# A post-norm transformer layer on eight cores: activation loads issued by ScalarE instead of GpSimd, and a scalar chain written as one row

## The reference

```python
# x: (8, 2048, 1024) f32, one sequence per core
# 1. causal attention with a low-rank K and V, then residual and layernorm
q = (x @ wq)                      # 8 heads of 128
k_lat = x @ wk_down; v_lat = x @ wv_down     # 2 KV heads, latent width 32
k = k_lat @ wk_up; v = v_lat @ wv_up
y = softmax(causal(q k^T / sqrt(128))) v     # 4 query heads share a KV head
x = layernorm(x + y @ wo)
# 2. six nodes, each with three edges and full attention of 8 heads
nodes = {-1: x}
for c in range(6):
    q = ew[c,0] * (nodes[in_q] @ We[eq] + be[eq])
    k = ew[c,1] * (nodes[in_k] @ We[ek] + be[ek])
    v = ew[c,2] * (nodes[in_v] @ We[ev] + be[ev])
    o = softmax((q Wq)(k Wk)^T / sqrt(128)) (v Wv) @ Wo
    nodes[c] = act_w[c] * o + q
# 3.
x = layernorm(x + layernorm(nodes[5]) * g + b)
```

## Time and profile before

| | |
|---|---|
| two runs | 7837.41 and 7932.83 us, median 7885.12 us |
| profiled execution | 7838.38 us, slowest core's span 7837.3 us |
| the eight cores' spans | 7800.0 to 7837.3 us |
| busy in the span: TensorE | 5592.8 us (71%) |
| ScalarE, VectorE | 2477.1 us (32%), 1753.2 us (22%) |
| mean granted TensorE clock | 0.852 of 2.4 GHz |
| DMA: issued by GpSimd (q0), by SyncE (q1) | 224.67 MB, 42.76 MB |

### The profile page before, as it was taken

One profiled execution on the slowest core, in us unless ns is written; L12 is line 12 of the kernel. 1 busy time (PEld: TensorE's weight loads), 2 busy tenths in 40 slices (PEclk: granted clock), 3 DMA queues, 4 the chain that ended last, 5 costly groups with the idle time before them and its releaser, 6 DMA issues.

```text
span 7837.3 us, 67298 instructions; the slowest of 8 cores (7800.0 to 7837.3 us)
## 1 busy us (share of the span) xinstructions
PE 5592.8 (71%) x21825; PEld 2141.0 (27%) x22250; DVE 1753.2 (22%) x2522; ACT 2477.1 (32%) x2138; POOL 127.8 (2%) x161
## 2 busy tenths in 40 slices
PE   6455668677886777867778967779777779656654
PEld 3111123222332223322223422224222234212211
DVE  2432222111112112131112131111311112332233
ACT  1123402454123452115440134431144511224322
POOL 0000000000000000000000000000000000000000
PEclk9577878899997998979898979989889989778777
DMA  3000031000330002310003300113200023000000
GB/s 81 11 27 27 17 91 33 17 11 11 70 65 6 19 15 49 97 27 11 11 11 81 76 16 11 22 38 76 54 17 11 11 59 94 10 17 11 27 27 22
DMA packets 112503, 271.76 MB, mean 35 GB/s; under 512 B 5216, under 2 KB 30112, under 8 KB 112182
## 3 DMA queue, kind: packets, MB, share of 16 engines
q0 software_dynamic: 98768, 224.67, 12.9%
q1 hardware_dynamic: 13414, 42.76, 1.6%
HBM read 286.55 MB, written 67.11 MB: 45 GB/s over the span
## 4 chain that ended last, share of the span: by engine, by line
PE 53%; ACT 21%; DVE 11%; issue 9%; DMA 5%; DVEq 1%; ACTq 0%; SPq 0%; POOLq 0%; POOL 0%
PE psS L57 26%; PE psA L57 20%; ACT Dm L57 16%; ACT rowb L57 5%; PE psY L57 4%; PE psM L57 3%; DVE LNw L57 3%; DVE rowb L57 3%; DVE Dm L57 2%; DMA A<-nsc 1%; DVE psS L57 1%; DMA x1w<-x 1%; DVE mask_sb L57 1%; DVE x1w L57 1%; DMA B<-x1b 1%
## 5 line engine op out<-in xcount | busy, mean ns | idle before, releaser
L57 ACT ACTIVATE Dm<-psS,negC 128x2048 bf16<-128x2048 f32 x848 | 1668.0, 1967 | 2099.4 <-PE psS L57 1906.5
L57 PE MATMUL psS<-A,B 128*128 128x512 bf16 x3282 | 900.0, 393 | 423.7 <-ACT Dm L57 395.4
L57 PE MATMUL psA<-Dm,Wb 128*128 128x512 bf16 (+1 forms) x2564 | 657.8, 411 | 108.6 <-DVE Dm L57 82.0
L57 DVE CAST mask_sb<-rowb 1x512 bf16<-1x512 f32 x192 | 79.7, 415 | 2911.4 <-ACT rowb L57 2911.4
L57 PE MATMUL psY<-Dm,Cv 128*128 128x512 bf16 x1651 | 498.1, 428 | 273.1 <-DVE Dm L57 224.4
L57 PE MATMUL psA<-Dm,Cv 128*128 128x512 bf16 x1654 | 495.1, 424 | 267.7 <-DVE Dm L57 221.1
L57 PE MATMUL psM<-Dm,on_b 128*1 128x512 bf16 x1808 | 542.4, 419 | 165.7 <-ACT Dm L57 158.4
L57 PEld LDWEIGHTS psS<-A,B 128*128 128x128 bf16 x3392 | 317.3, 98 | 1026.7 <-issue 881.8
L57 PE MATMUL psS<-Dm,Wb 128*128 128x512 bf16 (+1 forms) x2561 | 588.9, 379 | 3.3
L57 PE MATMUL psA<-Dm,on_b 128*1 128x512 bf16 (+1 forms) x1712 | 491.2, 412 | 11.9 <-DVE Dm L57 7.8
L57 PE MATMUL psA<-A,Wb 128*128 128x512 bf16 x1255 | 310.8, 402 | 180.8 <-DMA A<-nsc 141.7
(11 more groups left out here) (122 smaller groups left out, 3772.3 us busy)
## 6 DMA issues: line engine op xcount, KB each, us to landing
A<-nsc POOLq DMA_DIRECT2D x18, 2048.0 KB, 19.5
Wb<-ffn_We POOLq DMA_DIRECT2D x15, 2048.0 KB, 15.2
qsp<-Dm SPq DMA_DIRECT2D x6, 4096.0 KB, 24.4
Dm<-qsp POOLq DMA_DIRECT2D x24, 1024.0 KB, 10.8
nsc<-x1w POOLq DMA_DIRECT2D x20, 1024.0 KB, 8.8
x1w<-x POOLq DMA_DIRECT2D x32, 512.0 KB, 3.6
B<-x1b POOLq DMA_DIRECT2D x8, 2048.0 KB, 17.1
Wb<-ffn_Wv POOLq DMA_DIRECT2D x6, 2048.0 KB, 24.4
```

Of the source, the lines that this page charges most:

```text
L57: r = f(*a, **k)
```

## The change

There are two edits.

First, in `attn_norms` the Ln, the Exp and the add-and-clip work on one row of 8 numbers, where they worked 8 times on one number each.

```diff
+            npair = len(pairs_q)
             gEV.wait(SE)
-            for pair in pairs_q:
-                SE.activation(out=rowb[0:1, ccol + pair:ccol + pair + 1],
-                              in_=rowb[0:1, ccol + pair:ccol + pair + 1], func=AF.Ln,
-                              bias=sc_fm[0:1, 42:43])
-                gSE.wait(SE, gSE.n)
-                SE.activation(out=rowb[0:1, ccol + pair:ccol + pair + 1],
-                              in_=rowb[0:1, ccol + pair:ccol + pair + 1], func=AF.Exp,
-                              scale=0.5)
+            SE.activation(out=rowb[0:1, ccol:ccol + npair],
+                          in_=rowb[0:1, ccol:ccol + npair], func=AF.Ln,
+                          bias=sc_fm[0:1, 42:43])
+            gSE.wait(SE, gSE.n)
+            SE.activation(out=rowb[0:1, ccol:ccol + npair],
+                          in_=rowb[0:1, ccol:ccol + npair], func=AF.Exp, scale=0.5)
             gSE.wait(VE)
-            for pair in pairs_q:
-                VE.tensor_scalar(out=rowb[0:1, ccol + pair:ccol + pair + 1],
-                                 in0=rowb[0:1, ccol + pair:ccol + pair + 1],
-                                 scalar1=-40.0, scalar2=0.0, op0=OP.add, op1=OP.max)
+            VE.tensor_scalar(out=rowb[0:1, ccol:ccol + npair],
+                             in0=rowb[0:1, ccol:ccol + npair],
+                             scalar1=-40.0, scalar2=0.0, op0=OP.add, op1=OP.max)
```

```diff
             for tb in range(NTB):
-                src_ready[0].wait(GP, src_ready[1])
-                gPE.wait(GP, pr)
-                gSE.wait(GP)
-                GP.dma_start(out=A3[:, :, (tb % 2) * 1024:(tb % 2) * 1024 + 1024],
+                src_ready[0].wait(SE, src_ready[1])
+                gPE.wait(SE, pr)
+                SE.dma_start(out=A3[:, :, (tb % 2) * 1024:(tb % 2) * 1024 + 1024],
                              in_=fmv(src_dram)[:, :, tb * 1024:(tb + 1) * 1024]
                              ).then_inc(dEa[tb % 2].h, 16)
...
             for qb in range(NQB):
-                dSq.wait(GP, qsp_dma)
-                gEV.wait(GP)
-                gPE.wait(GP)
-                GP.dma_start(out=Dq, in_=fmv(qsp_t)[:, :, qb * 512:(qb + 1) * 512]
+                dSq.wait(SE, qsp_dma)
+                gEV.wait(SE)
+                gPE.wait(SE)
+                SE.dma_start(out=Dq, in_=fmv(qsp_t)[:, :, qb * 512:(qb + 1) * 512]
```

More of the change, by code:

```diff
@@ L667, in build_nc @@
                 s, v = stage_free[sl]
-                s.wait(GP, v)
-            GP.dma_start(out=stg, in_=x_in[tt * 128:(tt + 1) * 128, :]).then_inc(dX[sl].h, 16)
+                s.wait(SE, v)
+            SE.dma_start(out=stg, in_=x_in[tt * 128:(tt + 1) * 128, :]).then_inc(dX[sl].h, 16)
             dX[sl].n += 16
@@ L803, in build_nc @@
                     s, v = stage_free[sl]
-                    s.wait(GP, v)
-                gEV.wait(GP)
-                dSb.wait(GP)
-                dSf.wait(GP)
-                GP.dma_start(out=stg, in_=x_in[qb * 512 + tt * 128: qb * 512 + (tt + 1) * 128, :]
+                    s.wait(SE, v)
+                gEV.wait(SE)
+                dSb.wait(SE)
+                dSf.wait(SE)
+                SE.dma_start(out=stg, in_=x_in[qb * 512 + tt * 128: qb * 512 + (tt + 1) * 128, :]
                              ).then_inc(dX[sl].h, 16)
@@ L934, in build_nc @@
                 for tb in range(NTB):
[L935 to L938, removed]
+                    node_write_dma[ink][0].wait(SE, node_write_dma[ink][1])
+                    gPE.wait(SE, a_free[0])
+                    SE.dma_start(out=B3[:, :, (tb % 2) * 1024:(tb % 2) * 1024 + 1024],
                                  in_=fmv(node_src[ink])[:, :, tb * 1024:(tb + 1) * 1024]
@@ L1031, in build_nc @@
                     emit_ln(LNw, LNw, EPS_F, True)
[L1032 to L1036, removed]
+                    dSf.wait(SE)
+                    dSn.wait(SE)
+                    gEV.wait(SE)
+                    gPE.wait(SE)
+                    SE.dma_start(out=x1w[:, :, :],
                                  in_=fmv(x1f_t)[:, :, qb * 512:(qb + 1) * 512]
```

## The result

The changed kernel takes 7820.2 us in the median of 35 runs, the kernel before 7883.4 us in the median of 34. The ratio is 0.9918, with a 95% interval of 0.9893 to 0.9943: 0.8% faster, some 65 us, where 1.8% and 144 us were forecast. The median of 7820.2 us lies above the forecast's range, which ends at 7790. The forecast was made from 7838.4 us, the faster of two runs, and 45 us of the distance to 7694 are only that; the other 81 us are gain that did not come. Carried to the forecast's base the ratio gives some 7774 us, inside the range of 7640 to 7790, with less than half of the forecast gain.

The account below looks back on a forecast made before the run. The chain that ended last was taken as the bound, TensorE holding 53%; only TensorE's standstills were reachable. From 7838.4 us, -48 - 66 - 18 - 22 - 4 + 14 = -144 gave 7694 us, range 7640 to 7790.

Parts of the forecast that it names:

- Part 1: End of attn_norms: one row instruction replaces eight single-number ones, 6.85 us less per norm, -48 us over seven norms.
- Part 2a: V edge's first half, nodes 2 to 5: loaded before the output projection, its wait goes, 3.5 us stall remains; -66 us.
- Part 2b: Kernel start: weights asked for at once, x tiles loaded by ScalarE, first projection near 69 us; -18 us.
- 1.4 us per load: X loads from ScalarE instead of GpSimd: 1.0 us less to landing plus 0.4 us sooner issue.
- Part 2c: Layer A's sixteen x tile loads, -22 us, and four x1f loads, -4 us, by issuing from ScalarE.
- no faster for being another queue: Rival: loads from ScalarE's queue land no sooner; start gives 7, x tiles 6, time 7725; chance 0.12.
- Part 2d: Eleven exposed first halves at q, key and v edges, now beside the weight load: 1.3 us more each, +14 us.
- the two ends that were drawn: Bounds for the eleven exposed halves: -15 us if undisturbed, +147 us if served only after the weight load.
- qsp's row: DMA beside a weight load, 4096 KB in 24.4 us, taken as 12.2 us for each exposed 2048 KB half.
- The +69: Eleven exposed halves sharing with weights from their first packet: 6.3 us each, +69 in place of +14, time 7749.
- the sign of a worse sharing: Q and key edge first-half waits much above 18 us, against 13.5 expected, would show sharing worse than assumed.
- Part 2e: Dq loads issued by ScalarE ahead of each block's first exponential: cost nothing, 12 us if an issue took 1.5 us.

## Why the prediction was wrong, point by point

**Part 1 was right and not complete.** 6.85 us a norm were forecast and 6.7 measured, 47.1 us in all. The step that failed is the one behind it, that what follows the norms stays as it is. The attention blocks became 28 us longer, so the edit alone is worth some 20 us. No term of the sum had room for this: the blocks stood in it at nothing, without a reason given.

**Part 2a: the mechanism was right, the size was 10 us off.** The wait for A is gone, VectorE's wait for the nsc write is what is late next, and the stall is 4.78 us, not 3.5. The four gaps gave 44.8 us, the shorter passes another 11: 56 in place of 66. The nsc write of nodes 2 to 5, 8.6 to 8.8 us in the chain, is slower than the 7.60 of the earlier trace rows.

**Part 2b: the step "1.4 us per load" failed, and one was missing.** The weights were there in time, as forecast. But the x tile landed in 3.3 us, so a tile took 2.84 us in place of 3.25 (medians over the cores), not the forecast 2.57. And the transposes began later than the forecast's 27.7. The constants, which are loaded before anything else is done, landed later (start, us to landing, first before, then changed), as they do in every kernel here that asks for the weights at once:

```profile
4.68 6.51 DMA rowb<-ffn_act_w
```

```profile
4.42 9.40 DMA rowb<-ffn_act_w
```

With them TensorE's first instruction came at 14.7 us in place of 11.8. The x loads stood behind it, and the first transpose came at 30.8 in place of 24.0. The last tile was copied at 76.9 us, 1 us later than before (75.9): the quicker tiles only made up for the later start, and the gain of 10.4 us is the wait for the weights, which is gone, in place of 18.

**Part 2c: the same step.** The store's 2.6 us did not carry over to a load; the tile gave 0.3 us by landing and about 0.4 by ScalarE's quicker start: 10.9 us in place of 22. The rival "no faster for being another queue", with -6, was nearer. The Trainium skill's "DMA: Bandwidth & Descriptors", section "Issuing engines are not separate DMA queues", says that only the time to initiate is saved, and this is borne out: a 2048 KB load with the weights behind it took 10.2 us from ScalarE and 10.5 us from GpSimd.

**Part 2d: mis-sized, +38 in place of +14.** The result lies between the two ends that were drawn, and the value was taken too near the lower. I went by qsp's row, whose store begins ahead of the weights. In the traces the half shares from the start: with the weights in another queue and ahead, it took 21.7 to 22.6 us, twice the 10.5 of before; with the weights a little behind it, 10.4 to 17.5. The Trainium skill's rule of turns between the queues ("DMA: Bandwidth & Descriptors", "Queues, rings and completion order") agrees with this, and with 1026 packets of the one queue beside 1191 of the other. The +69 that I had worked out for it and kept beside the sum was too much by 31, as +14 was too little by 24. The mean waits became 15.3 us at the q edges and 16.5 at the key edges, where 13.5 was forecast and 18 was named as the sign of a worse sharing. In nodes 0 and 1 the diff itself showed that the weight load passes the half, by 7 us of the nsc write; the forecast gave these two the same 1.3 us as the rest, and they alone cost 21.

**Part 2e was right.** 0.37 us on ScalarE's queue, nothing waits for it, and with Dq on GpSimd the time is the same.

**By cases.** The 28 us of the blocks, 24 us of the sharing, 11 of the x tiles, 10 of the v edges and 8 of the start make up the 81 us between 144 and 63. The range was too narrow because it held no case in which a gain of time is itself the cause of a loss. That the time came out within 2% of the kernel before, to which 0.59 was given, is in part luck: the largest single piece that brought it there, the 28 us, was in none of the cases.

## What to carry to other kernels

When a load that an engine waits for and a prefetch that it does not need yet come out of one queue into two, the order between them is lost: make the prefetch wait for the first half of the load (here 56 us), or issue the load where nothing stands ahead of it (here a further 100 us or so, by the q and key edges' gaps). A load is hidden by its place in the order of its issuer; changing the issuer pays by what no longer stands ahead, hardly by speed. And a kernel whose TensorE clock is granted below full speed in a regular pattern may lose elsewhere, by the changed length of the stretch ahead, what an edit gains: a sum over untouched stages shows it.

## What the runs showed of the hardware

The blocks of attention, with the same instructions and the same work of ScalarE and VectorE, took 126.6 us at a granted clock of 0.93 and 130.6 us at 0.90, and often the same to 0.1 us on all eight cores. Which of these a block takes changed with the time that the norm ahead of the blocks takes: 6.7 us less in each of seven places made 28 us more in the sum, 1.9 us more in each made 22 more, and with the old duration all came back. Shifts put at the start of the program, of 4.5 to 22 us, moved the sum by only 5 to 12 us. So the length of the stretch just ahead matters, and the place in the whole program hardly. How the one sets the pattern of the clock is not shown by these runs. The forecast had taken the clock of the untouched stages as fixed.
